# Decoder layer on one core: packing the weighed sums and repeating the scan output by DMA, and moving the router's count and exponential two slots on

## The reference, cut to what matters

```
x:   16 sequences x 256 tokens x 256 features, all float32
mixer:      xz = x W_in^T + b;  xh = silu(causal conv of 4 taps);  u = xh W_ssm^T + b
            h = h A^T + u B;  s = h C          (a scan: one number s per token)
            y = (s * xh + D * xh) * silu(gate);  x = layernorm(x + x + y W_out^T + b)
attention:  16 heads of 16 features, q from x, k and v from ctx, 256 x 256 scores a head
            out = softmax(q k^T / 4) v;  x = layernorm(x + out Wo^T + b)
experts:    probs = softmax(x Wr) over 8 experts; each token goes to its best expert,
            if it is among the first 640 of it; relu(t W1) W2, times the probability
            x = layernorm(x + that)
```

## Time and profile before

| | |
|---|---|
| median of 3 runs | 1017.08 us (1014.64 to 1022.38) |
| the profiled execution, its own time | 1020.84 us |
| its span, first to last instruction | 1019.1 us |
| granted TensorE clock, mean | 0.909 of 2.4 GHz |
| `mixer_in`, about | 0 to 140 us |
| `attend`, turns 4 to 14 | 265.46 to 618.45 us, 11 turns |
| `attend`, all | about 140 to 733 us |
| `experts`, about | 733 to 1019 us |

### The profile page before, as it was taken

One profiled execution on the slowest core, in us unless ns is written; L12 is line 12 of the kernel. 1 busy time (PEld: TensorE's weight loads), 2 busy tenths in 40 slices (PEclk: granted clock), 3 DMA queues, 4 the chain that ended last, 5 costly groups with the idle time before them and its releaser, 6 DMA issues. The chain is left out here.

```text
span 1019.1 us, 16854 instructions
## 1 busy us (share of the span) xinstructions
PE 863.1 (85%) x5964; PEld 663.5 (65%) x5964; DVE 597.7 (59%) x1441; ACT 405.0 (40%) x623; POOL 354.1 (35%) x290
## 2 busy tenths in 40 slices
PE   5998947789899888988989888887279999999993
PEld 4776725455666566655666556544279999999993
DVE  4889751545675777667676666643235555555542
ACT  4565611145444444445444454443043334233320
POOL 0333352222233434344342443223212442244422
PEclk9999967679998999999999998877579999999997
DMA  3117302444443445444344442400343222343100
GB/s 115 42 43 210 108 24 78 113 106 126 104 126 115 109 111 125 124 113 114 103 124 121 117 114 74 116 21 24 106 135 109 94 88 90 113 128 106 46 22 22
DMA packets 73432, 98.82 MB, mean 97 GB/s; under 512 B 10529, under 2 KB 60874, under 8 KB 73376
## 3 DMA queue, kind: packets, MB, share of 16 engines
q1 hardware_dynamic: 69920, 89.95, 32.0%
q0 software_dynamic: 3456, 8.13, 2.2%
HBM read 63.40 MB, written 35.73 MB: 97 GB/s over the span
## 5 line engine op out<-in xcount | busy, mean ns | idle before, releaser
L946 DVE TENSOR_REDUCE nmax<-ps_m 128x4 f32<-128x1024 f32 x128 | 156.6, 1224 | 174.6 <-PE ps_m L711 172.1
L903 ACT ACTIVATE pt<-ps_a 128x1024 f32<-128x1024 f32 x128 | 131.1, 1025 | 89.7 <-PE ps_a L721 88.3
L1216 ACT ACTIVATE hid<-ps_h 128x640 fp32r<-128x640 f32 x64 | 45.1, 705 | 151.3 <-PE ps_h L1156 151.3
L1156 PE MATMUL ps_h<-xt,w_hi 128*128 128x320 f32 x512 | 99.9, 318 | 1.0 <-DVE xt L1231 1.0
L1168 PE MATMUL ps_y<-w_hi,hid 128*128 128x256 f32 x640 | 85.3, 284 | 1.7 <-issue 1.7
L1265 DVE SCALAR_TENSOR_TENSOR hid<-ps_h,hid 128x640 fp32r<-128x640 f32 x64 | 52.7, 824 | 56.2 <-ACT hid L1216 55.7
L1156 PEld LDWEIGHTS ps_h<-xt,w_hi 128*128 128x128 f32 x512 | 80.0, 191 | 5.5 <-DVE hid L1265 3.9
L1168 PEld LDWEIGHTS ps_y<-w_hi,hid 128*128 128x128 f32 x640 | 80.1, 192 | 1.9 <-issue 1.9
L721 PE MATMUL ps_a<-qst,kst 49*128 49x256 f32 x512 | 67.8, 345 | 15.5 <-ACT pt L903 15.2
L721 PEld LDWEIGHTS ps_a<-qst,kst 49*128 49x128 f32 x512 | 40.8, 197 | 57.0 <-issue 31.8
L711 PE MATMUL ps_m<-kst,qst 48*128 48x256 f32 x512 | 66.9, 342 | 11.1 <-DVE nmax L946 5.9
(11 more groups left out here) (169 smaller groups left out, 1654.9 us busy)
## 6 DMA issues: line engine op xcount, KB each, us to landing
halves_dram<-half SPq DMA_DIRECT2D x64, 256.0 KB, 2.4
gated<-in_w SPq DMA_DIRECT2D x16, 1024.0 KB, 5.4
kst<-halves_dram SPq DMA_DIRECT2D x64, 128.0 KB, 3.1
qst<-halves_dram SPq DMA_DIRECT2D x64, 128.0 KB, 3.2
rows_dram<-blank SPq DMA_DIRECT2D x1, 5160.0 KB, 19.7
gated<-rows_dram SPq DMA_DIRECT2D x8, 645.0 KB, 4.2
x_raw<-in_x_t SPq DMA_DIRECT2D x8, 512.0 KB, 3.9
xres<-in_x SPq DMA_DIRECT2D x16, 256.0 KB, 3.6
```

What stands on the lines that cost most here:

```text
L903: nc.scalar.activation(pt[:, k % 4].rearrange("p s t q -> p (s t q)"), ps_a[:].rearrange("p s t q -> p (s t q)"), ACT.Exp).then_inc(s["exp ...
L946: nc.vector.tensor_reduce(nmax[:, q, :, :, h // 2].rearrange("p t s -> p s t"), ps_m[:], AX.X, ALU.max, negate=True).then_inc(s["max_done" ...
L1156: mm = pe.matmul(ps_h[:, f % 2, c2, 0:HC], w1[a][:, p, k, f * P:(f + 1) * P], xt[:, b, p, k, c2 * HC:(c2 + 1) * HC], start=(n == 0 and k = ...
L1216: nc.scalar.activation(hid[:, HI, f, :].rearrange("p (c n) -> p c n", c=2), ps_h[:, f % 2, :, 0:HC], ACT.Relu).then_inc(s["hid_hi"], 1)
```

## The change: what it does

1. The weighed sums are not transposed any more. In `vals` the value columns stand on both sides of the ones, so for head groups 0 and 1 the sums lie in the lower and for groups 2 and 3 in the upper 16 rows of a head's 32. SP packs them by transfers from SBUF to SBUF (`part`): all sums into `odim`, all sums of weights into `osum`, both with features on partitions. A half of a sequence takes 8 transfers of 16 partitions x 2 KB, so there are 16 more a turn. The second half (`part(n-3, .., 1)`) stands between the stores of k and q, the first half (`part(n-2, .., 0)`) behind the load of ctx.
2. In slot 9 VectorE takes the reciprocal of the whole of `osum` (128 x 512) in place and multiplies it with `odim` (128 x 512) into `ont`. `project_out` comes in slots 11 and 12 (were 12 and 13). `sums_by_query`, the second `turn`, the copies by line 887 and lines 1028 and 1029 are gone. Wv's and Wo's layouts are permuted to fit.
3. The scan output is transposed once at the end of `mixer_in`, written to DRAM in four transfers, and one transfer a turn (`load_s`) brings a sequence's 256 numbers to all partitions (`sb`, two buffers). `diag` and `spread_s` are gone; `y` reads `sb` in slot 11 (was 13), and `mixer_out` comes in slots 13 and 14 (were 14 and 15).
4. `count` moves from slot 6 to 8 on TensorE, its VectorE work two slots on, and the exponential `el` on ScalarE from slot 5 to slot 7. `r2` and its statistics come one slot earlier (13 and 14).
5. SP no longer waits for the landing of k before it stores q; it waits for both before the stacking.

```
+            sp.wait_ge(st_ready, 1)
+            for cq in range(4):
+                sp.dma_start(dram["scan"].rearrange("b (q c i) -> q b c i", q=4, c=4)[cq],
+                             c["s_rows"][B * cq:B * (cq + 1), :].rearrange("p (c n) -> p c n", c=4)[:, :, 0:L]
+                             ).then_inc(c["scan_out"], 16)
...
+            pe.wait_ge(s_ready, 1)
+            pe.wait_ge(gate_ready, MH * NG)
+            pe.wait_ge(c["loaded"], 16 * len(c["loads"]))
+            pe.transpose(ps_gate[0:4 * B, 0, 0:P], s_all[:].rearrange("p c b -> p (c b)"), c["eye"][:]
+                         ).then_inc(st_mm, 1)
...
+            dve.wait_ge(st_mm, 1)
+            nc.vector.tensor_copy(c["s_rows"][:], ps_gate[0:4 * B, 0, 0:P]).then_inc(st_ready, 1)
+            dve.wait_ge(st_ready, 1)
...
+            def load_s(j, p):
+                settled(sp)
+                need(sp, s["y_done"], j - 1)
+                sp.dma_start(sb[:, p], dram["scan"][bass.ds(j, 1), :].to_broadcast([P, S])).then_inc(s_in[p], 16)
...
+            def part(j, p, side):
+
                 settled(sp)
-                sp.wait_ge(stored, j * 32 + 32)
-
+                sp.wait_ge(s["oraw_hi" if side else "oraw_lo"], j + 1)
+                need(sp, s["ont_out"], j)
+                for i in range(PV):
+                    rows = slice(NP * HD // 2 * side + HD * i, NP * HD // 2 * side + HD * (i + 1))
+                    for tile, odd in ((odim, side), (osum, 1 - side)):
+                        first = VW * i + HD * odd
+                        sp.dma_start(tile[rows, :, :], oraw[first:first + HD, 2 * side:2 * side + 2, :]
+                                     ).then_inc(o_in[side][p], 16)
+
+            sp.wait_ge(c["scan_out"], 64)
+            load_s(0, 0)
             load_x(0, 0)
             load_ctx(0, 0)
...
+                if on(n, -2):
+                    load_s(n + 2, p)
...
+                if on(n, 3):
+                    part(n - 3, 1 - p, 1)
+                if on(n, 0):
                     store(n, p, 1, s["q_split"], s["q_stored"])
+                    settled(sp)
+                    sp.wait_ge(s["k_stored"], n * 32 + 32)
+                    sp.wait_ge(s["q_stored"], n * 32 + 32)
                     stack(n, p, 0)
                 if on(n, 0) and on(n, -1):
...
+                if on(n, 2):
+                    part(n - 2, p, 0)
...
-            def spread_s(j):
-                pe.wait_ge(s["diag_done"], j + 1)
-                need(pe, s["v_out"], j - 1)
-                need(pe, s["q_out"], j)
-                pe.matmul(ps_d[:, 0:S], ones[:], diag[:].rearrange("p c i -> p (c i)"), start=True, stop=True
-                          ).then_inc(s["sbc_mm"], 1)
...
-                        mm = pe.matmul(ps_o[VW * i:VW * (i + 1), g, :], vals[:, p, t, h, :],
+                        odd = g // 2
+                        mm = pe.matmul(ps_o[VW * i:VW * (i + 1), g, :],
+                                       vals[:, p, t, g % 2 * PV + i, HD * odd:HD * odd + VW],
...
-            def sums_by_query(j, t):
-                if t == 0:
-                    pe.wait_ge(s["oraw_hi"], j + 1)
-                    need(pe, s["place_done"], j)
-                else:
-                    pe.wait_ge(s["on_done"], 2 * j + 1)
-                for g in range(4):
-                    mm = pe.transpose(ps_e[:, g * P:(g + 1) * P], oraw[:, g, t * P:(t + 1) * P], eye[:])
-                mm.then_inc(s["ot_mm"], 1)
...
-                    if h == 12 and on(n, -1):
-                        spread_s(n + 1)
-                    if h in (14, 15) and on(n, -1):
-                        mixer_out(n + 1, h - 14)
+                    if h in (13, 14) and on(n, -1):
+                        mixer_out(n + 1, h - 13)
...
-                    if h == 6 and on(n, 4):
+                    if h == 8 and on(n, 4):
                         count(n - 4)
-                    if h in (7, 9) and on(n, 3):
-                        sums_by_query(n - 3, (h - 7) // 2)
-                    if h == 11 and on(n, 3):
-                        pe.wait_ge(s["on_done"], 2 * (n - 3) + 2)
-                        turn(ps_e, onrm, s["ont_mm"])
-                    if h in (12, 13) and on(n, 3):
-                        project_out(n - 3, h - 12)
+                    if h in (11, 12) and on(n, 3):
+                        project_out(n - 3, h - 11)
                     if h == 1 and on(n, 4):
...
+            def sums_out(j, p, half_of, done):
 
                 act.wait_ge(s["pv_mm"], NG4 * j + NG4 // 2 * (half_of + 1))
-                need(act, s["ot_mm"], 2 * j)
+                if not isinstance(j, int) or j > 0:
+                    act.wait_ge(o_in[half_of][1 - p], use(j - 1, OIN, 1 - p))
...
-                    if h == 5 and on(n, 4):
+                    if h == 7 and on(n, 4):
...
-                    if h == 12 and on(n, 3):
-                        act.wait_ge(s["ont_mm"], n - 2)
-                        nc.scalar.copy(ont[:].rearrange("p k t -> p (k t)"), ps_e[:]).then_inc(s["ont_out"], 1)
...
-                    if h in (8, 10) and on(n, 3):
-                        t = (h - 8) // 2
-                        dve.wait_ge(s["ot_mm"], 2 * j + t + 1)
-                        if t == 0:
-                            need(dve, s["ont_mm"], j)
-                        o4 = ps_e[:].rearrange("p (h w) -> p h w", w=VW)
-                        oc.done(nc.vector.reciprocal(rec[:], o4[:, :, HD]))
-                        nc.vector.tensor_tensor(onrm[:, t].rearrange("p (h d) -> p h d", d=HD), o4[:, :, 0:HD],
-                                                rec[:, :, None].to_broadcast([P, NH, HD]), ALU.mult
-                                                ).then_inc(s["on_done"], 1)
-                    if h == 14 and on(n, 3):
+                    if h == 9 and on(n, 3):
+                        dve.wait_ge(o_in[0][q], use(j, OIN, q))
+                        dve.wait_ge(o_in[1][q], use(j, OIN, q))
+                        need(dve, s["oproj_mm"], j)
+                        oc.done(nc.vector.reciprocal(osum[:], osum[:]))
+                        nc.vector.tensor_tensor(ont[:], odim[:], osum[:], ALU.mult).then_inc(s["ont_out"], 1)
...
-                    if h == 7 and on(n, -1):
-                        need(dve, s["sbc_mm"], n + 1)
-                        nc.vector.tensor_tensor(diag[:], s_all[:, :, bass.ds(n + 1, 1)].to_broadcast([P, 4, 64]),
-                                                mask[:, None, :].to_broadcast([P, 4, 64]), ALU.mult
-                                                ).then_inc(s["diag_done"], 1)
-                    if h == 13 and on(n, -1):
-                        dve.wait_ge(s["sbc_mm"], n + 2)
+                    if h == 11 and on(n, -1):
+                        dve.wait_ge(s_in[q], use(n + 1, 16, q))
+                        need(dve, s["wout_mm"], n + 1)
                         for m in range(MH):
-                            op = nc.vector.scalar_tensor_tensor(y[:, m, :], ps_d[:, 0:S], c["d_col"][:, m:m + 1],
+                            op = nc.vector.scalar_tensor_tensor(y[:, m, :], sb[:, q], c["d_col"][:, m:m + 1],
                                                                 gated[:, m, bass.ds((n + 1) * S, S)], ALU.add, ALU.mult)
                         op.then_inc(s["y_done"], 1)
```

More of the change, by code:

```diff
@@ L391, in attend @@
     VW = 2 * HD
+    VP = 3 * HD
     AL, WL = 3, 5
@@ L398, in attend @@
     ctx = T("ctx", [P, 2, KD, S], F32)
-    diag = T("diag", [P, 4, 64], F32)
+    sb = T("sb", [P, 2, S], F32)
     y = T("y", [P, MH, S], F32)
@@ L451, in attend @@
     KIN, QIN = 4 * 16, 4 * 16
+    o_in = [[s["lo_in0"], s["lo_in1"]], [s["hi_in0"], s["hi_in1"]]]
+    OIN = 2 * PV * 16
     FIRST, LAST = 6, B - 3
@@ L672, in mixer_out @@
                     pe.wait_ge(s["y_done"], j + 1)
+                    need(pe, s["v_out"], j - 1)
+                    need(pe, s["q_out"], j)
                 for m in range(MH):
@@ L1007, in step @@
                         nc.vector.tensor_tensor(carry[:], carry[:], hot[:, 0, :], ALU.add).then_inc(s["place_done"], 1)
-                    if h == 7 and on(n, 4):
+                    if h == 9 and on(n, 4):
                         dve.wait_ge(s["sel_out"], n - 3)
@@ L1012, in step @@
                         nc.vector.tensor_tensor(carry[:], carry[:], hot[:, 1, :], ALU.add).then_inc(s["carry_ready"], 1)
-                    if h == 8 and on(n, 4):
+                    if h == 10 and on(n, 4):
                         dve.wait_ge(s["place_out"], n - 3)
@@ L1353, in load @@
                 return tile
-            c["s"] = hold("s_all", [P, 4, B])
+            c["s_rows"] = hold("s_rows", [4 * B, P])
+            dram["scan"] = nc.dram_tensor("scan_dram", (B, S), F32, kind="Internal").ap()
             c["blank"] = hold("blank", [P, ROW])
@@ L1362, in decoder @@
             c["bv_rep"] = load("bv_rep", [P, KD, P], "(k p) n -> p k n", p=P)
```

(12 more changed lines are left out.)

42 lines of the change are left out of this document (24 added, 18 removed).

## The result

| | before | after |
|---|---|---|
| median, us | 1017.21 | 1041.58 (1037.94 to 1045.4) |
| ratio, 95% interval | 1 | 1.0234 (1.0177 to 1.029) |
| profiled execution, us | 1020.8 | 1043.2 |
| its span, us, and granted clock | 1019.1, 0.909 | 1041.4, 0.886 |

What follows compares the result with a forecast made beforehand. TensorE, busy 85% of the span, was taken to set the pace. From 1020.8 us, -18 for twelve full turns and +0.5 elsewhere gave 1003.3 for the profiled execution; the median forecast was 1001, range 970 to 1033.

Steps and rivals of the forecast that it cites:

- The count and the exponential: Moved two slots on, they let TensorE's queries start 2.08 us earlier; less 0.25 for the count, gain 1.83 us.
- Transposes and spread: Removing the weighed sums' transposes, the turn back and the spread takes 3.23 us a turn off TensorE's list.
- the turn of 25.9 us without a wait: A full turn at full clock, 30.98 - 1.83 - 3.23 us, before any new wait is added.
- The issue of a transfer: SP issues each `part` transfer in 0.45 us, like the stacking, so eight take 3.6 us.
- Landing: Data of the second half's transfers are there 2.2 us after issue ends, at 474.1.
- The reciprocal: VectorE's 128x512 reciprocal, extrapolated from rows of 128x2 and 128x16, takes 3.3 us.
- Rival (b): The reciprocal takes 4.4 us: +1.1 us a turn in 13 turns, 1015 us, no change; chance 0.16.
- The wait for `ont`: TensorE stands idle 3.2 us before `project_out` in every turn, waiting on the chain SP, DMA, VectorE.
- The clock: The new gap brings the low clock level at least as often, costing 1.4 us a turn: 30.6 against 32.09.
- SP "just in time, no room": SP's list grows by 17 transfers, about 7.7 us a turn; the row of maxima is just in time.
- The end: In turns 17 and 18 no scores cover the chain: +0.8 us and +4.0 us.
- Rival (a): Transfers cost 0.68 us each to issue: wait over 5 us, turn 32.8, median 1029 us; chance 0.22.

Runs made afterwards that it cites:

- e1: The kernel before with only the count and its exponential moved two slots on; 980.87 us, ratio 0.9641.
- e11: The kernel after with a copy for the wide reciprocal and the transfers writing `osum` left out, so the layer is not computed; 951.2 us, ratio 0.9321.
- e13: The kernel after with 9 useless TensorE products put ahead of its wait for `ont`; 1028.05 us, ratio 1.0059.
- e9: The kernel after with SP's turn begun by the row of maxima and the stacking, ahead of output, `load_s` and load of x; 1036.97 us, ratio 1.0157.
- e3: The kernel before with count and exponential two slots on and the scan output repeated by a transfer, `y` still in slot 13; 999.14 us, ratio 0.9818.

## Why the prediction was wrong, step by step

Three terms of the sum failed: the issue time of a transfer, taken at 0.45 us; the price of the clock behind the wait, taken at 1.4 us a turn; and SP's full list, which was named and put at nothing. The chain itself, its order and its place in the turn were as forecast.

**The count and the exponential**, 1.83 us: right for the work, 2.04 at full clock in e1. On the kernel before they gave 2.9 a turn with the clock. I gave the whole clock gain to the last line of the sum, but it belongs to whatever removes idle time.

**Transposes and spread** at 3.23 us, and the turn of 25.9 us without a wait: right within 0.2 by e11's turn at full clock (26.06), and 0.8 low by its mean turn (26.71), of which 0.45 are waits for q's transfers (0.03 in after).

**The issue of a transfer**, taken at 0.45 us: failed. The transfers stand 0.63 us apart (0.59 and a gap), eight take 5.0 us instead of 3.6. The bound of 0.68 from the row of maxima was the near one; I had preferred the stacking for its shape of 16 partitions. My reading of the rule of the Trainium skill that put `part` at the stacking's price ("DMA: Bandwidth & Descriptors", section "Why a DMA increments its semaphore by 16 and not by 1") is refuted by the same rows: 16 partitions on the outer dimension, and still 0.59. What the row of maxima and `part` share is that both ends lie in SBUF; that this is the cause was not tried by itself.

**Landing** of 2.2 us: 550.79 - 549.32 = 1.5 from the end of the last issue, as the forecast counted it (from its start it is 2.0, here and in the median over all). **The reciprocal** at 3.3 us from two short rows: 3.35 in 16 instances. Rival (b) is refuted, and with it my reading of the repeat count in the Trainium skill ("VectorE: DVE Perf Modes", section "First, the fixed hardware budget") as 4.4 us.

**The wait for `ont`**, 3.2 us: measured 4.06 in the turn shown, 0.86 more, and 3.98 on the mean. The transfers give 1.4 of that and the landing takes 0.7 back; the rest is within 0.2.

**The clock**, 1.4 us a turn: too low, though by how much is less sure. e13 against after gives 1.5 to 1.9. What is left of 32.61 when the turn without wait, 3.98 for `ont` and 0.19 for the row are taken off is 1.7 with e11's mean turn and 2.4 with its turn at full clock; that remainder holds whatever else I did not see. I had carried over the price of 1.1 that several gaps of 2.5 us in all had the earlier trace rows, and widened it by a little for the longer one. What I did not look at is where the lower clock falls: behind this wait stand the projection, whose four products take 1.3 to 2.1 us instead of 1.03, and then `mixer_out`.

**SP "just in time, no room"**: named in the prediction and given no price. In full turns it costs 0.19 us on the mean. In turn 3 the row is copied at 235.43 and issued at 237.80:

```profile
237.80 1.40 SPq L572 DMA_DIRECT2D qst<-mrow  x2
```

```profile
243.82 0.51 PE L763 MATMUL ps_a<-qst,kst 49*128 49x256 f32 x4 [3.47 <-DMA qst<-mrow]
```

Turn 3 has this wait and one of 4.04 for `ont`, and its granted clock is 0.83: +9.4 us where I had -2. Turn 17 has 3.53 and 3.88 of the same kinds. e9 shows 3.7 us of turn 3's loss to be SP's order.

**The end**: from the end of `oraw` in turn 18 to `r` it takes 739.91 - 725.28 = 14.6 us, +5.1 where I had +4.0.

**The sum again.** A full turn took 2.0 us more than the 30.6 of the forecast. The longer wait is 0.8 of that and the row 0.2. The other 1.0 is divided between the clock (0.1 to 0.5 by e13) and the turn without wait (0.1 to 0.7 by e11), and the runs do not divide it further. By stretch, measured against mine: eleven turns +5.7 instead of -16.5, turn 3 +9.4 instead of -2, the stretch behind the full turns +9.6 instead of about +1.3, what lies ahead of turn 3 -2.5 instead of -0.3. The differences are 22.2, 11.4, 8.3 and -2.2, and 1003.3 + 39.7 = 1043.0; the profiled execution took 1043.2. Rival (a) had the right direction and named the issue time as what decides. Its 32.8 us a turn is partly luck: it had 0.68 an issue (0.63 measured), a wait of over 5 us (4.0) and the low clock at 1.7, and its errors cancel. Its 1029 fell 12 us short, for want of turn 3.

## What to carry to other kernels

Work taken from the busiest engine is worth what it measures only if nothing late stands in its place: here 3.2 us of transposes and spread were removed in each turn and 4.0 us of waiting put there, and the clock behind the wait costs another 1.5 to 1.9 us (e13). Where two rows disagree on the price of a new transfer, price it by both and let the forecast carry both; here the row between the same memories (0.68) was nearer to the 0.59 to 0.63 measured than the one of the same shape (0.45). Count the whole list of the queue in the turns that have no slack, the first and the last. Try the small part alone: moving the count and the exponential two slots on was worth 36 us, and the rest of the change, with its chain cut down as in e11, could have won 30 more (951 against 981).

## What the runs showed of the hardware

Idle time of TensorE is dearer than it looks: nine useless products in the place of a wait of 4.0 us, which they did not shorten, made the kernel 13.5 us faster by the medians (1041.58 to 1028.05) and 18 by the ratios (1.0234 to 1.0059), with a granted clock of 0.99 in the full turns instead of 0.91. A transfer from SBUF to SBUF of 16 partitions occupied SP's queue for 0.59 us (the median of 128), those between SBUF and DRAM in the same kernel for medians of 0.37 to 0.47. And VectorE's operations with both operands in SBUF took up to 2.2 us instead of 0.47 beside GpSimd's additions (e3), and stayed at 0.48 or less with one operand in PSUM (before).
